# Fillers between score blocks, expert slots swapped over in half of the hidden units, and results read back in blocks: a change to a vision-tower kernel

## The reference, cut to what matters

```python
q, k, v = (silu(x @ W) for W in (Wq, Wk, Wv))
energy = jnp.einsum('bhnd,bhmd->bhnm', q, k) * decay
out = jnp.einsum('bhnm,bhmd->bhnd', energy, v)
out = _layernorm((out * gate) @ Wo, ln_w, ln_b)
...
logits = jnp.einsum('sd,btd->bst', sl, tok)
dispatch_w = jax.nn.softmax(logits, axis=-1)
combine_w = jax.nn.softmax(logits, axis=-2)
y = jnp.einsum('btd,bst->bsd', xn, dispatch_w)
y = jnp.einsum('sio,bsi->bso', fc1_weight, y) + fc1_bias
y = jax.nn.gelu(y, approximate=False)
y = jnp.einsum('sio,bsi->bso', fc2_weight, y) + fc2_bias
out = jnp.einsum('bsd,bst->btd', y, combine_w)
```

## Time and profile before

| | us |
|---|---|
| median of 3 runs | 1350.14 (1349.92 to 1350.39) |
| the profiled execution, its own time | 1349.98 |
| its span, first to last instruction | 1348.2 |
| TensorE busy (products) | 1219.4 (90%) |
| VectorE busy | 784.1 (58%) |
| ScalarE busy | 711.3 (53%) |
| GpSimd busy | 565.2 (42%) |

### The profile page before, as it was taken

How to read it: one execution, slowest core, us unless ns; L and a number is a source line. 1 busy time by engine, 2 the same in 40 slices (tenths; PEclk the granted TensorE clock), 3 DMA queues, 4 the chain that set the end, 5 groups by cost and what they waited for, 6 DMA issues and landing times.

```text
span 1348.2 us, 34010 instructions
## 1 busy us (share of the span) xinstructions
PE 1219.4 (90%) x12578; PEld 972.2 (72%) x12578; DVE 784.1 (58%) x2049; ACT 711.3 (53%) x1613; POOL 565.2 (42%) x846
## 2 busy tenths in 40 slices
PE   5999999999999999999999999999978999997563
PEld 4788888888888888888888888888854555554332
DVE  4666666666666666666666666666661111111797
ACT  5456666666665666666666566666642111110466
POOL 5254455444555445544455544554430000000564
PEclk8999999999999999999999999999987999999555
DMA  4412111111112111111111211111162999993886
GB/s 154 159 62 70 51 48 48 48 48 48 48 48 72 68 51 48 48 48 48 48 48 48 72 68 51 48 48 57 74 235 89 367 367 373 367 352 92 233 262 190
DMA packets 50708, 158.33 MB, mean 117 GB/s; under 512 B 5370, under 2 KB 31344, under 8 KB 38384
## 3 DMA queue, kind: packets, MB, share of 16 engines
q1 hardware_dynamic: 33072, 145.04, 30.9%
q10 hardware_dynamic: 17600, 12.78, 3.1%
HBM read 132.18 MB, written 25.62 MB: 117 GB/s over the span
## 4 chain that ended last, share of the span: by engine, by line
PE 79%; DVE 15%; issue 1%; DMA 1%; ACT 1%; SPq 1%; DVEq 1%; POOL 0%; ACTq 0%; POOLq 0%
PE ps L908 9%; PE ps L909 8%; PE ps L910 8%; DVE p_sb L773 7%; PE ps L967 7%; PE ps L938 6%; PE ps L1002 6%; PE ps L1166 5%; PE ps L1182 4%; PE ps L1186 4%; PE ps L1045 3%; PE ps L950 3%; PE ps L951 2%; PE ps L985 2%; PE ps L1068 2%; PE ps L1195 2%
## 5 line engine op out<-in xcount | busy, mean ns | idle before, releaser
L409 POOL TENSOR_TENSOR xl<-x_sb,xh 128x392 fp32r<-128x392 f32 x192 | 190.1, 1031 | 211.6 <-DVE gn L748 203.2
L773 DVE TENSOR_TENSOR p_sb<-ps,dec 98x1176 f32<-98x1176 f32 x128 | 176.9, 1382 | 84.4 <-PE ps L967 84.4
L967 PE MATMUL ps<-qm,kT 32*98 32x196 f32 x1536 | 117.0, 343 | 39.0 <-DVE p_sb L773 39.0
L967 PEld LDWEIGHTS ps<-qm,kT 32*98 32x98 f32 x1536 | 75.2, 158 | 70.4 <-DVE p_sb L773 58.3
L631 ACT ACTIVATE hg<-ps 128x768 f32<-128x768 f32 x32 | 25.9, 811 | 184.8 <-PE ps L1186 184.8
L712 DVE BATCH_NORM_STATS2 st<-ps 98x6 f32<-98x192 f32 x128 | 40.1, 355 | 129.9 <-PE ps L938 129.9
L1002 PE MATMUL ps<-p_sb,vpad 98*32 98x98 f32 x3072 | 112.4, 250 | 0.8 <-DVE p_sb L773 0.8
L1002 PEld LDWEIGHTS ps<-p_sb,vpad 98*32 98x32 f32 x3072 | 84.5, 109 | 34.3 <-issue 33.0
L873 DVE COPY y2st<-ps 128x192 f32<-128x192 f32 x32 | 11.5, 358 | 155.7 <-PE ps L1166 155.7
L938 PE MATMUL ps<-wo,og 96*98 96x192 f32 x512 | 93.7, 325 | 0.0
L496 POOL CAST pickb<-pick 128x128 fp32r (+1 forms) x32 | 9.4, 294 | 192.1 <-PE ps L1186 192.1
(11 more groups left out here) (174 smaller groups left out, 3379.9 us busy)
## 6 DMA issues: line engine op xcount, KB each, us to landing
x_sb<-in_xT SPq DMA_DIRECT2D x32, 1176.0 KB, 5.7
w1v<-in_fc SPq DMA_DIRECT2D x32, 1152.0 KB, 7.6
w2v<-in_fc SPq DMA_DIRECT2D x32, 1152.0 KB, 9.9
h_dram<-h SPq DMA_DIRECT2D x32, 294.0 KB
h2r<-h_dram SPq DMA_DIRECT2D x32, 294.0 KB
out<-o_sb ACTq DMA_DIRECT2D x32, 294.0 KB
comb_dram<-cst SPq DMA_DIRECT2D x32, 98.0 KB, 1.7
cbuf<-comb_dram SPq DMA_DIRECT2D x32, 98.0 KB, 3.9
```

Of the source, the lines that this page charges most:

```text
L409: pool.tensor_tensor(xl[:, k], x_sb[:, k], xh[:, k].bitcast(F32), ALU.subtract)\
L773: dve.tensor_tensor(dst, src, rate.unsqueeze(2).to_broadcast([T, PAIRS, 2, TOK]), ALU.mult)\
L967: mm = pe.matmul(ps[0:T, SC_AT + r, mt * TOK:(mt + 1) * TOK].rearrange("p (b n) -> p b n", b=2), kT[rows, g, n], qm[rows, g, :, n], start= ...
```

## The change

In phase 1, `logits_turned` stands in front of `scores(i, 1)` in the steps that have both, where it stood before the key projection; `slot_maxima` moves with it on VectorE, behind `kts`. `carried(i, 0)` and `carried(i, 1)` stand before `scores(i, 3)`, where they stood behind `values(i, 2)`; `gated(i, 0)` moves to before `decay(i, 3)` on VectorE, and GpSimd makes `qd` before `split_x`. In phase 2, the two slots of a pair exchange their 64 output partitions in the second half of the hidden units, the four products of 64 by 64 follow one another, `pickb` gets a third column block (a second small copy on GpSimd), and results have three buffers in place of two. Before phase 3, `cbuf` and `h2r` lie outside the ring places and are issued without the wait for 30 pairs, and `y2r` is read in three blocks of slot pairs (0 to 25, 26 to 29, 30 and 31), each when its results are stored.

```diff
+READY = (NU - RING, NU - REST, NU)
+Y2 = 3
...
-            sp.wait_ge(fc2_mm, RING * TURNS)
             sp.wait_ge(h2_stored, 16 * NP)
             sp.wait_ge(comb_stored, 16 * NP)
             for n in range(DEEP):
                 load_comb(n, n)
                 load_h2(n, n)
-            for par in range(2):
-                sp.wait_ge(y2_stored[par], 16 * NU // 2)
-            for n in range(DEEP):
-                c = slice(n * NP // DEEP, (n + 1) * NP // DEEP)
+            sp.wait_ge(fc2_mm, RING * TURNS - 2)
+            for u0, u1 in zip((0,) + READY[:-1], READY):
+                for m in range(Y2):
+                    sp.wait_ge(y2_stored[m], 16 * ((u1 - m + Y2 - 1) // Y2))
                 for a in range(2):
-                    sp.dma_start(y2r[64 * a:64 * a + 64, c, :], y2_dram[:, a, c, :]).then_inc(y2r_loaded[n], 16)
+                    rows = slice(64 * a + 2 * u0, 64 * a + 2 * u1)
+                    sp.dma_start(y2r[rows, :, :], y2_dram[2 * u0:2 * u1, a]).then_inc(y2r_loaded, 16)
...
-            pool.wait_ge(y2r_loaded[0], 32)
+            pool.wait_ge(y2r_loaded, 32 * len(READY))
...
-                if d:
+                if d and not a:
                     logits_turned(i - 2)
...
                     gate(i)
+                    if d:
+                        logits_turned(i - 2)
                     scores(i, 1, c)
...
                 if a:
+                    carried(i, 0)
+                    carried(i, 1)
                     scores(i, 3, c)
                     values(i, 2)
-                    carried(i, 0)
-                    carried(i, 1)
...
+            def half_of(s, x):
+                return s if x == 0 else 1 - s
...
                     for s in range(2):
-                        pe.matmul(ps[64 * s:64 * s + 64, x, 0:FH], y_u[:, u, s], w1v[n][:, s, f],
-                                  start=False, stop=False)
+                        at = 64 * half_of(s, x)
+                        pe.matmul(ps[at:at + 64, x, 0:FH], y_u[:, u, s], w1v[n][:, s, f], start=False, stop=False)
+                for x in range(2):
+                    f = slice(x * FH, (x + 1) * FH)
                     for s in range(2):
-                        half = slice(64 * s, 64 * s + 64)
-                        mm = pe.matmul(ps[half, x, 0:FH], yT1[half, u], w1v[n][half, 2, f],
+                        at, half = 64 * half_of(s, x), slice(64 * s, 64 * s + 64)
+                        mm = pe.matmul(ps[at:at + 64, x, 0:FH], yT1[half, u], w1v[n][half, 2, f],
                                        start=False, stop=True)
```

More of the change, by code:

```diff
@@ L49 @@
 STAGE_AT = 4 * 24832
+SLOT = 3 * F + 2 * FJ * D
+READY = (NU - RING, NU - REST, NU)
+Y2 = 3
+assert RING % Y2 == 0
 BANK = 512
@@ L138, in vit_tower @@
         hgT = place("hgT", [128, FJ, 128])
-        y2st = place("y2st", [128, 2, D])
+        y2st = place("y2st", [128, Y2, D])
         for n in range(RING):
@@ L144, in vit_tower @@
             w2v.append(place(f"w2v{n}", [128, 2, FJ, D]))
-        place = placer(region_at)
+        slot_at = [region_at + 4 * (2 * F + Y2 * D + n * SLOT) for n in range(EARLY)]
+        place = placer(slot_at[REST])
         y2r = place("y2r", [128, NP, D])
-        place = placer(region_at + 4 * (2 * F + 2 * D) + REST * 4 * (3 * F + 2 * FJ * D))
+        place = placer(slot_at[EARLY - 1] + 4 * SLOT)
         cbuf, h2r = place("cbuf", [128, DEEP, TOK]), place("h2r", [T, DEEP, 4, D])
+        place = placer(region_at + STAGE_AT)
         y2b = place("y2b", [128, DEEP, D])
@@ L232, in vit_tower @@
         tr_mm, hgT_rdy, fc2_mm, y2st_rdy = (sem(n) for n in ("tr_mm", "hgT_rdy", "fc2_mm", "y2st_rdy"))
-        y2_stored = [sem("y2_stored0"), sem("y2_stored1")]
+        y2_stored = [sem(f"y2_stored{n}") for n in range(Y2)]
         h2r_loaded = [sem(f"h2r_loaded{n}") for n in range(DEEP)]
-        y2r_loaded = [sem(f"y2r_loaded{n}") for n in range(DEEP)]
+        y2r_loaded = sem("y2r_loaded")
         cbuf_loaded = [sem(f"cbuf_loaded{n}") for n in range(DEEP)]
@@ L435, in step @@
                     first_norm(i - 1, 1)
-                if more:
-                    if c:
-                        pool.wait_ge(gn_rdy, 4 * i)
-                    split_x(i + 1, range(KP))
                 if a:
@@ L445, in step @@
                             .then_inc(qd_rdy, 1)
+                if more:
+                    if c:
+                        pool.wait_ge(gn_rdy, 4 * i)
+                    split_x(i + 1, range(KP))
                 if c:
@@ L495, in slot_step @@
                 src = pick[:, :].rearrange("p (u s) -> p u s", s=2)
-                pool.tensor_copy(pickb[:, n % 2], src[:, u].unsqueeze(2).to_broadcast([128, 2, NB])).then_inc(pick_rdy, 1)
+                pool.tensor_copy(pickb[:, n % 2, 0:2], src[:, u].unsqueeze(2).to_broadcast([128, 2, NB]))\
+                    .then_inc(pick_rdy, 1)
+                pool.tensor_copy(pickb[:, n % 2, 2:3], src[:, u, 0:1].unsqueeze(2).to_broadcast([128, 1, NB]))\
+                    .then_inc(pick_rdy, 1)
             phase2(pool, slot_step)
@@ L506, in bias @@
                 pool.tensor_tensor(y2b[:, n], y2r[:, p], b2[:, :], ALU.add).then_inc(y2b_rdy, 1)
-            pool.wait_ge(y2r_loaded[0], 32)
+            pool.wait_ge(y2r_loaded, 32 * len(READY))
             for n in range(DEEP):
                 bias(n, n)
-            for n in range(1, DEEP):
-                pool.wait_ge(y2r_loaded[n], 32)
             with pool.Fori(0, NP // DEEP - 1) as w:
@@ L846, in step @@
                                       ALU.mult).then_inc(kts_rdy, 1)
+                    if d:
+                        slot_maxima(i - 2)
                     decay(i, 1)
@@ L856, in step @@
                     decay(i, 2)
-                if a:
+                    gated(i, 0)
                     decay(i, 3)
-                    gated(i, 0)
                     gated(i, 1)
@@ L864, in slot_step @@
             def slot_step(u, n, v):
-                par = n % 2
+                m = n % Y2
                 dve.wait_ge(tr_mm, u + 1)
@@ L868, in slot_step @@
                     .then_inc(hgT_rdy, 1)
-                if not (isinstance(u, int) and u < 2):
-                    dve.wait_ge(y2_stored[par], 16 * (RING // 2 * v + n // 2))
+                if not (isinstance(u, int) and u < Y2):
+                    dve.wait_ge(y2_stored[m], 16 * (RING // Y2 * v + n // Y2))
                 dve.wait_ge(fc2_mm, u + 1)
-                dve.tensor_copy(y2st[:, par], ps[:, 4 + par, 0:D]).then_inc(y2st_rdy, 1)
+                dve.tensor_copy(y2st[:, m], ps[:, 4 + n % 2, 0:D]).then_inc(y2st_rdy, 1)
             phase2(dve, slot_step)
```

17 lines of the change are left out of this document (9 added, 8 removed).

## The result

| | before | after |
|---|---|---|
| median | 1350.03 us (1349.29 to 1350.39, 4 runs) | 1306.35 us (1304.31 to 1307.93, 4 runs) |
| span of the profiled execution | 1348.2 us | 1306.2 us |
| its time | 1349.98 us | 1307.93 us |
| full step of phase 1 | 30.65 us | 29.94 us |
| slot pair in phase 2 | 6.63 us | 5.85 us |

The ratio is 0.9676 (95% interval 0.966 to 0.9693): 43.7 us less, where 45.3 were forecast. The time is right, but of the four terms under it only that of the products in phase 2 is: phase 1 gave 7.2 us less than forecast, and the supply and the tail cost 1.0 and 3.1 us less. The misses have opposite signs, and more than half of them cancels; that part is luck.

What follows compares the result with a forecast made beforehand. TensorE was taken to bound phase 1, with two holes a step, and phase 2 without a hole, DMA close behind. -27.0 - 26.0 + 1.0 + 6.6 = -45.4 us from 1349.98 gave 1304.6, median 1304.7; range 1290 to 1320.

Steps and rivals of the forecast that it cites:

- phase 1: Term for moving work into TensorE's waits: 0.90 us for each of 30 full steps, -27.0 us.
- the products in phase 2: Term for the experts' 64 by 64 products: a group costs 0.79 us once, not twice; -26.0 us, slot pair 5.84 us.
- the supply: Term for phase 2 weight loads: at 379 GB/s a slot pair needs 6.5 us against 5.84; stall of +1.0 us.
- the tail: Term after the last `fc2_pair`: third residual sum 27.4 us after its end against 20.8, +6.6 us.
- the holes: TensorE's two gaps per phase 1 step, 0.67 and 0.54 us, before `scores` blocks waiting for VectorE's decay.
- Both fillers: `logits_turned` and the two `carried`, moved into phase 1's 0.67 and 0.54 us gaps; 0.61 + 0.29 us a step.
- what could be late next: Phase 1 check: key projection's second half needs `zs`, ready at 518.67 and wanted at 518.83.
- the lower bound of 20.7 us: Smallest phase 1 gain given: 0.49 + 0.20 = 0.69 us a step; the upper was 1.00, 30.0 us.
- The model of the ring: Phase 2 weight buffers: a lead of 16.0 us shrinks 0.66 us a load, 16.5 over 25, emptied almost exactly at the end.
- the tail shrinks: Rival on the end: result rows go at engine rate, tail 15.4 us, -5.4 instead of +6.6; 1292.7 us, chance 0.20.
- The quarters: Rival in phase 2: four array quarters do not run at once, gain only 5.4 us; 1314.7 us, chance 0.13.
- The granted clock: Rival in phase 2: TensorE's clock falls while waiting for weights, some 5.4 us more per slot pair; slower, chance 0.03.

Runs made afterwards that it cites:

- fillers alone: Kernel before with only the change's phase 1 moves (`logits_turned`, `carried`, gated products), experts' phase as before: 1328.78 us (0.9843).
- logits alone: Kernel before with only `logits_turned` ahead of group 1's scores and the decay's maxima moved with it; carried products left in place: 1340.45 us (0.994).
- eighth run: Changed kernel without the experts' four 64 by 64 products (last 64 of 192 first-layer features left out), all transfers unchanged: 1299.73 us (0.9627).
- seventh run: Changed kernel with ScalarE's two copies to `zs` made ahead of its copies to `qm` and `qs` of group 1: 1296.19 us (0.9601).
- fourth run: Changed kernel with results reloaded as before: eight reads of 64 partitions after all stores; three result buffers stay: 1304.33 us (0.9663).
- tenth run: As the fourth run, but each quarter of the columns read in one transfer of 128 partitions instead of two of 64: 1351.82 us (1.0014).
- ninth run: Changed kernel with each early read of results cut into four by columns, rows of 6.1 KB instead of 24.6 KB: 1298.96 us (0.9623).

## Why the prediction was right, and where only its sum was

| term | forecast | measured | by |
|---|---|---|---|
| phase 1, a full step | -0.90 us | -0.71 us | 30.65 to 29.94, also with the fillers alone |
| of it `logits_turned` | -0.61 | -0.35 | logits alone |
| of it `carried` | -0.29 | -0.36 | fillers less logits |
| phase 1 | -27.0 | -19.8 | first L1191 at 1002.73, L1179 at 1022.49; -21.0 as the average of the executions with each phase 1 |
| phase 2, products | -26.0 | -25.8 | first bias product to the start of the last `fc2_pair` as due: 215.03 to 189.27; slot pair 5.85 |
| supply stall | +1.0 | 0 | no wait |
| tail | +6.6 | +3.5 | 26.5 less 22.99 |
| sum | -45.4 | -42.1 | 1307.93 less 1349.98, the two profiled executions; the medians say -43.7 |

Phase 1 missed by 7.2 us, and the supply and the tail by 4.1 the other way. Had only phase 1 been wrong, the forecast would have been 7 us off. The time came out close in part by luck.

**Phase 1: the holes were read rightly, the cover was not.** Both fillers lie in the holes; what they gained fell short by what `zs` cost. The step that failed is the sentence on "what could be late next": it gave `zs` a margin of 0.16 us and counted it as enough. I had dated the product by the chain, 0.16 us later than it starts, and had left out its weight load, one product ahead, and the 0.22 us from `zs` to that load. In the prediction's own numbers: wanted by the chain at 518.83, by the timeline at 518.67, its weight load at 518.50, and `zs` is ready at 518.67. The margin was negative before the change was made. `logits_turned` had been the cover that hid it. With `zs` early the three pieces are 0.35, 0.36 and 0.29: 1.00 us a step, the upper bound that I gave. Without that, the whole phase came out at the lower bound of 20.7 us: 19.8 between these two executions, 21.0 on average. Before's own trace had the gap where no logits stand ahead, in the first steps; I did not look there. The chain of waits of the kernel before:

```profile
60.60 0.18 PE ps L910
60.78 0.10 issue
60.87 0.39 PE ps L908
```

**Phase 2** came as forecast, for the reason given.

**The supply: the rate was mis-sized.** I took a DMA share of 0.98 for saturation and so 371/0.98 = 379 GB/s for the most. But 371 GB/s is 2.46 MB in 6.63 us, what TensorE asked for, and the landings were short. The ceiling is 425 GB/s (eighth run). The model of the ring held there within two loads. With this ceiling the lead does not shrink at 5.85 us; it would below 5.78. The Trainium skill (DMA: Bandwidth & Descriptors, Specifications) gives about 358 GB/s as a core's DRAM limit; 425 GB/s, measured here on one core, are 19% above it.

**The tail: the sign was right, the reason partly.** Forecast were 12.7, 6 and 6 us for the three blocks, one after another behind the weights. A's rows took 17.6 us to move (1176.0 to 1193.6) and C, from its second issue, 7.5: slower than forecast. And they do not stand in one line: B and C each waited for a store, C for that of the late last product. The loss is smaller than forecast because the last weights landed some 20 us before the last `fc2_pair` was to end (issued 1161.3 and landed 12.9 later, against 1194.2), not 9.1: without a stall the reads had more time. What I did not see at all is that A delays the stores on the other queue, so that a third buffer is not enough, and VectorE's copy holds `hgT` and the last product (4.2 us here, 1.2 in the seventh run's execution). Six buffers take that away, and 2.25 of the 3.5 us with it; rows cut to 6.1 KB take all of it and 5.7 us more (17.3 us against 22.99). The rival "the tail shrinks" gave a long row an engine of its own and 1.06 us; C's rows, with nothing beside them, took 1.8 to 2.9 us each, four at a time.

**The other rivals.** The quarters do run at once. The granted clock did not fall within the slot pairs (1.00 in every window from 1020 to 1190); it fell in the wait before the last product and stayed down while the reads ran (0.50, the lower of its two levels, from 1205 to 1210).

Still open: why the reads of results go at 230 to 268 GB/s at a share of 1.00 where weights go at 425. A row of 6.1 KB took 0.44 us (median) in the fourth run, with some 15 under way, and 0.23 in the tenth with two; a weight row of 9.2 KB took 0.35 with 15 under way. In the ninth run a window had 310 GB/s (1180 to 1185). The second queue gave little, and whether the half of the partitions sets the rate was not isolated. The prediction's estimate for block C by the ports that the Trainium skill counts (SBUF — State Buffer, Door 1: The DMA port swizzle) was 7.2 us, and 7.5 were measured. That does not test the rule: by the packets C moved in 5.8 us, four rows at a time.

## What to carry to other kernels

Before a piece of work is moved, read which wait it covers where it stands: look in the trace for a place where the piece is missing (first steps, last steps), and ask for the margin at the weight load, one product ahead, plus 0.2 us. A DMA share near 1 is a ceiling only if the rate is not simply the demand; the landing times say which. An early read is only early if its rows do not hold up what it depends on: transfers of 52 rows of 24.6 KB kept another queue's stores from landing for up to 20 us, and the same bytes in rows of 6.1 KB did not.

## What the hardware showed unasked

- A transfer of 128 partitions whose source has an outermost count of two moved at a share of 0.13, two of sixteen DMA engines, and 53 GB/s (tenth run).
- Transfers of 4 rows of 24.6 KB, two of them with nothing beside them, had four rows under way at once: 34 GB/s, 1.8 to 2.9 us a row.
- A store of 96 KB on one queue landed after 20.3 us in place of 7.5 (the store issued at 1161.5) while rows of 24.6 KB from another queue were under way; with rows of 6.1 KB after 8.7 at most.
- Weights, and the stores beside them, moved at 421 to 425 GB/s on one core for 140 us (eighth run).
- A weight load that waits on a semaphore began 0.22 us after its releaser ended (509.84 to 510.06, and 60.62 to 60.84 in the kernel before), and the product behind it took 0.39 us in place of 0.18.
- Four 64 by 64 products on the four quarters took 0.81 us, as long as two on two quarters (0.79).
